# One graph-network kernel, one core: gathers gated per tile and on the preparation's products, window one-hots made in smaller pieces

## The reference, cut to what matters

```python
# first layer: relational graph convolution
msg = sum_b (x[src] @ weight[b]) * w_comp[etype][:, b]        # 8 bases
agg = relu(segment_sum(msg * norm, dst) + bias)
x1  = layernorm(x + agg)
# second layer: messages with edge features, then an MLP with batch norm
neigh = segment_sum(x1[src] + edge_feat, dst)
h   = relu(batchnorm(((1 + eps) * x1 + neigh) @ W1 + b1))
out = layernorm(x1 + h @ W2 + b2)
```

## Time and profile before

| | us |
|---|---|
| median of 3 runs (780.35 to 783.78) | 781.75 |
| the profiled execution, its own time | 781.48 |
| its span in the trace | 779.7 |

### The profile page before, as it was taken

The page is one execution under the profiler, slowest core; times in us unless marked ns, Lnnn a source line. Parts: engine busy times, 40 slices in busy tenths (PEclk is TensorE's granted clock), DMA queues, the critical chain, the costliest instruction groups (busy, mean ns, idle before and its releaser), DMA issues.

```text
span 779.7 us, 13302 instructions
## 1 busy us (share of the span) xinstructions
PE 585.2 (75%) x3971; PEld 480.7 (62%) x3971; DVE 493.7 (63%) x1866; ACT 297.0 (38%) x672; POOL 418.9 (54%) x434
## 2 busy tenths in 40 slices
PE   4137877777878686888678877797787876999994
PEld 2025766655667574776556766666676665878764
DVE  7039666667569676777764887767774344536456
ACT  9502444544455444445443544345340000000074
POOL 6730767667667665766765666666656666100000
PEclk9998657677875788757889788999889888999998
DMA  4400335455454654545744647566565562463002
GB/s 115 108 25 2 99 117 147 119 158 149 133 145 119 189 170 149 163 131 161 217 134 126 203 136 221 167 200 200 153 199 161 181 203 71 126 240 129 2 1 83
DMA packets 97035, 108.21 MB, mean 139 GB/s; under 512 B 10805, under 2 KB 81446, under 8 KB 96962
## 3 DMA queue, kind: packets, MB, share of 16 engines
q1 hardware_dynamic: 80898, 79.25, 32.6%
q0 software_dynamic: 13312, 27.29, 12.8%
q10 hardware_dynamic: 2752, 0.79, 0.4%
HBM read 81.73 MB, written 25.56 MB: 138 GB/s over the span
## 4 chain that ended last, share of the span: by engine, by line
DVE 34%; PE 34%; another core or an unknown queue 12%; issue 10%; DVEq 4%; ACT 3%; DMA 1%; ACTq 0%; SPq 0%
PE psum L1053 11%; DVE etype_hot L1388 7%; PE psum L999 6%; DVE etype_hot L1385 5%; PE psum L1029 5%; PE psum L1005 5%; DVE sums_flat L1509 5%; PE psum L1020 3%; DVE adj_flat L1479 3%; DVE weighted L1307 3%; DVE adj_flat L1283 2%; DVEq L1482 1%; ACT adj_flat L804 1%; DVE sums_flat L1463 1%
## 5 line engine op out<-in xcount | busy, mean ns | idle before, releaser
L716 POOL DMA_INDIRECT gathered_flat<-in_x_dram,src_i x416 | 416.6, 1001 | 247.3 <-issue 106.2
L999 PE MATMUL psum<-weighted,gathered_flat 128*128 128x160 f32 (+1 forms) x832 | 178.0, 342 | 23.4 <-issue 21.0
L999 PEld LDWEIGHTS psum<-weighted,gathered_flat 128*128 128x128 f32 x832 | 156.6, 238 | 42.1 <-issue 39.7
L1509 DVE TENSOR_TENSOR sums_flat<-psum,sums_flat 128x180 f32 x208 | 71.9, 346 | 168.8 <-remote 90.8
L1020 PE MATMUL psum<-etype_hot 128*128 128x300 f16 (+2 forms) x624 | 119.2, 313 | 48.4 <-issue 26.2
L778 ACT ACTIVATE adj_flat<-zero_col 128x450 f16<-128x450 f32 x208 | 108.4, 579 | 107.9 <-DMA adjacency<-adj_flat 66.6
L1005 PEld LDWEIGHTS psum<-hot,attrs 128*128 128x128 f32 x832 | 136.5, 231 | 9.5 <-issue 9.4
L1005 PE MATMUL psum<-hot,attrs 128*128 128x20 f32 (+1 forms) x832 | 131.0, 273 | 7.7 <-issue 7.7
L1388 DVE TENSOR_SCALAR etype_hot<-iota_key,key_t 128x300 f16<-128x300 f16 (+1 forms) x416 | 131.9, 318 | 0.0
L1020 PEld LDWEIGHTS psum<-etype_hot 128*128 128x128 f16 x624 | 69.7, 132 | 68.9 <-issue 43.0
L1385 DVE TENSOR_SCALAR etype_hot<-iota_key,gathered_flat 128x128 f16<-128x128 f16 x416 | 108.8, 262 | 0.1
(11 more groups left out here) (144 smaller groups left out, 345.6 us busy)
## 6 DMA issues: line engine op xcount, KB each, us to landing
attrs<-in_edge_attr_dram SPq DMA_DIRECT2D x51, 512.0 KB
adjacency<-adj_flat SPq DMA_DIRECT2D x26, 900.0 KB
sums_flat<-adjacency SPq DMA_DIRECT2D x13, 576.0 KB
gathered_flat<-in_x_dram,src_i POOLq DMA_INDIRECT x416
coef<-adjacency SPq DMA_DIRECT2D x23, 288.0 KB
sums_flat<-adjacency SPq DMA_DIRECT2D x5, 648.0 KB, 8.8
sums_flat<-adjacency SPq DMA_DIRECT2D x9, 288.0 KB
out_dram<-gathered_flat SPq DMA_DIRECT2D x6, 256.0 KB
```

The costliest lines, as they stand in the source:

```text
L716: pool.indirect_dma_start(gathered[:, t % (RING * GROUP), :], None, x[:, :], bass.IndirectOffsetOnAxis(src_i[:, t:t + 1], 0)).then_inc(gat ...
L999: nc.tensor.matmul(ps[:, 0:B, STARTS[i]:STARTS[i] + WIDTHS[i]], gathered[:, (u * UNIT + i) % (RING * GROUP), 0:F], weighted_tiles(s, i)[:, ...
L1509: nc.vector.tensor_tensor(window, unit_psum(u), window, ALU.add).then_inc(added, 1)
```

## The change

Four edits. (1) In the preparation POOL's gathers of units 8 to 15 each wait for a number of finished coefficient quads: 26 (u - 7) // 8, that is 3, 6, 9, ... 26. (2) In the main loop each gather waits for its own tile: each tile's gather product (L999) adds one to a new semaphore `tiles_read`, and the gather of tile t waits for t - 31 of them. (3) DVE makes place one-hots for a couple (2 tiles per instruction) and weighted ones for a unit (1 tile per instruction), spread over the couples: after couple w the ones of couple w + 4, between the halves of the keys. (4) `select_ready` counts units, PE waits for it at each unit, and SP's waits are scaled to it.

```diff
@@ sync: loads into coef
-                        sp.wait_ge(select_ready, (place - NEARS - FARS + 1) * FREE_COEF)
+                        sp.wait_ge(select_ready, (place - NEARS - FARS + 1) * FREE_COEF * GU)
...
-                        sp.wait_ge(select_ready, GROUPS)
+                        sp.wait_ge(select_ready, U)
@@ gpsimd
             def gather_unit(u):
 
-                if u >= RU:
-                    pool.wait_ge(sums_mm, (u - RU) // 2 + 1)
                 for t in range(u * UNIT, (u + 1) * UNIT):
+                    if u >= RU:
+                        pool.wait_ge(tiles_read, t - RU * UNIT + 1)
                     pool.indirect_dma_start(
...
             for u in range(RU):
+                if u >= RU // 2:
+                    pool.wait_ge(coef_mm, QUADS * (u + 1 - RU // 2) // (RU // 2))
                 gather_unit(u)
@@ tensor: sums_of_unit
-                        pe.wait_ge(select_ready, g + 1)
+                    pe.wait_ge(select_ready, u + 1)
...
-                                         start=(i == 0), stop=(i == UNIT - 1))
+                                         start=(i == 0), stop=(i == UNIT - 1)).then_inc(tiles_read, 1)
@@ vector
-            def places_hot(g, s):
-
+            def places_hot(w):
+
+                g, lo = 2 * w // GU, 2 * w % GU
                 for i, n in enumerate(WIDTHS):
+                    t = 2 * w * UNIT + i
                     last = nc.vector.tensor_tensor(
-                        hot_tiles(s % 2, i),
-                        rel_t[:, g * GROUP + i:(g + 1) * GROUP:UNIT].unsqueeze(2).to_broadcast([P, HALF, n]),
-                        iota_win[:, 0:n].unsqueeze(1).to_broadcast([P, HALF, n]), ALU.is_equal)
+                        hot_tiles(g % 2, i)[:, lo:lo + 2, :],
+                        rel_t[:, t:t + 2 * UNIT - i:UNIT].unsqueeze(2).to_broadcast([P, 2, n]),
+                        iota_win[:, 0:n].unsqueeze(1).to_broadcast([P, 2, n]), ALU.is_equal)
                 last.then_inc(hot_ready, 1)
 
-            def weight_hot(g, s):
-
-                dve.wait_ge(hot_ready, g + 1)
+            def weight_hot(u):
+
+                g, j = u // GU, u % GU
+                dve.wait_ge(hot_ready, u // 2 + 1)
                 for i, n in enumerate(WIDTHS):
+                    t = u * UNIT + i
                     last = nc.vector.tensor_tensor(
-                        weighted_tiles(s % 2, i), hot_tiles(s % 2, i).unsqueeze(2).to_broadcast([P, HALF, B, n]),
-                        coef[:, g * GROUP + i:(g + 1) * GROUP:UNIT, :].unsqueeze(3).to_broadcast([P, HALF, B, n]),
+                        weighted_tiles(g % 2, i)[:, j, :, :], hot_tiles(g % 2, i)[:, j, :].unsqueeze(1).to_broadcast([P, B, n]),
+                        coef[:, t:t + 1, :].rearrange("p t b -> p (t b)").unsqueeze(2).to_broadcast([P, B, n]),
                         ALU.mult)
                 last.then_inc(select_ready, 1)
...
-            for g in range(2):
-                places_hot(g, g)
-                weight_hot(g, g)
+            for w in range(GU):
+                places_hot(w)
+                for u in range(2 * w, 2 * w + 2):
+                    weight_hot(u)
...
-                    for c in range(min(U, counted(2 * w - 2) + KEYRING), min(U, counted(2 * w) + KEYRING)):
-                        keys_hot(c)
+                    if w + GU < COUPLES:
+                        places_hot(w + GU)
+                    fresh = range(min(U, counted(2 * w - 2) + KEYRING), min(U, counted(2 * w) + KEYRING))
+                    for j in range(2):
+                        for c in fresh[:(len(fresh) + 1) // 2] if j == 0 else fresh[(len(fresh) + 1) // 2:]:
+                            keys_hot(c)
+                        if w + GU < COUPLES:
+                            weight_hot(2 * (w + GU) + j)
...
-                    if w % 2 == 1 and g + 2 < GROUPS:
-                        places_hot(g + 2, g)
-                        weight_hot(g + 2, g)
```

More of the change, by code:

```diff
@@ L406, in gnn_resnorm_kernel @@
         sums_mm = sem("sums_mm")
+        tiles_read = sem("tiles_read")
         added = sem("added")
```

## The result

On the chip of the first measurement the changed kernel takes 778.66 us (median of 13 runs, 774.6 to 784.0), the kernel before 783.10 (13 runs). The ratio is 0.9946 [0.9924, 0.9968]: 4.4 us faster, where 28 were forecast. The profiled execution took 777.41 us, its span is 775.6.

The account below looks back on a forecast made before the run. The prediction took POOL's back-to-back gathers, which hold back PE's reports, to set the main loop's beat. Its terms, -16 + 1 - 27 + 14 = -28 us from 781.5, gave 753.5 us, with a range of 712 to 782.

Parts of the forecast that it names:

- (3) The wait per tile: Main loop: each gather waiting for its own tile lengthens gather runs to 11.6, so fewer stops; -27 us.
- (2) The first one-hots: Start of PE's block products: first unit about 1 us sooner, but the keys behind its one-hots later; +1 us.
- (4) The smaller pieces: DVE in the main loop: more, smaller one-hot instructions add 23 to 57 us of work, mostly covered by idling; +14 us.
- (1) The gate: Preparation: gathers 17 to 32 waiting for quads let PE's reports through earlier; -16 us, ends 10 and 22.
- Rival (d): Preparation: the gate does nothing, late gathers hold the quads just as long and only shift; 781 us, chance 0.07.
- rival (c): Main loop: POOL wakes at the first report, so runs get short and the kernel slower; 802 us, chance 0.11.
- Rival (a): Only the preparation gains; in the main loop DVE's extra work eats what POOL gains; 766 us, chance 0.20.
- (b): Main loop: single-tile waits free PE's reports often enough that half of the 107 us of stops goes; 711 us, chance 0.15.

Follow-up runs that it names:

- split_3: Kernel before with only the smaller one-hots at their earlier place in the couple, and the matching waits: 794.5 us against 774.7, ratio 1.0249.
- gate_3: Kernel before with only the preparation's gathers 17 to 32 waiting for coefficient quads: 758.8 us against 774.7, ratio 0.9807.
- tile_3: Kernel before with only the main loop's wait per tile: 767.2 us against 774.7, ratio 0.9897.
- no_gather: Kernel before without the main loop's gathers, PE multiplying the rows the preparation brought: 690.7 us against 780.2, ratio 0.8848.
- gate_2: Kernel before with only the preparation's gathers 17 to 32 waiting for coefficient quads, on a faster chip: 667.1 us against 667.7, ratio 0.9988.
- tile_only: Kernel before with only the main loop's wait per tile, on a faster chip: 666.8 us against 666.6, ratio 1.0008.
- tile_2: Kernel before with only the main loop's wait per tile, again on a faster chip: 666.2 us against 667.7, ratio 0.9966.
- group_early: Kernel before with its group-sized one-hots, unchanged, moved ahead of keys, block additions and shared columns: 784.4 us against 775.1, ratio 1.0114; repeated, 1.0150.
- split_last: Kernel before with the smaller one-hots, placed at the couple's end where the group-sized ones stood: 784.4 us against 775.1, ratio 1.0113.

## Why the prediction was wrong

Its direction was right and its size was not: 4.4 us for 28, the profiled run 777.4 for 753.5. Of the 24 us between them, about 20 are term (3) and 5 are terms (2) and (4) together. By its own terms, for chips of kind B:

**(1) The gate, -16: right.** Alone it measures -15.9. The quads resumed at 29 us (DVE's row after its last wait, 29.23 in the trace of after), the pairs recurred each 3.3 us instead of the feared 4.1, and the first product moved by 18.8 us, between the ends of 10 and 22. Rival (d) is out. On kind A, where there is no hold, the same edit gives nothing.

**(2) The first one-hots, +1: about right.** The first product came a little sooner (70.98 for 72.44 us in split_3), but the second unit 5.6 us after it (53.65, 59.25), where gate_3 has 3.3:

```profile
53.60 1.29 PE L1001 MATMUL psum<-weighted,gathered_flat 128*128 128x160 f32 x4 [3.27 <-DVE weighted L1309]
...
56.85 1.19 PE L1001 MATMUL psum<-weighted,gathered_flat 128*128 128x160 f32 x4
```

That is 1.5 us sooner and 2.3 later; in time it is part of the split's 19.8.

**(3) The wait per tile, -27: the step that failed.** It measures -7.5 on kind B and nothing on kind A. The step took a run of gathers plus a stop as the beat of the loop, filled the run up with the tiles that the old wait rounds away, to 11.6, and called the rest gain. The runs did not fill up: in tile_3 they are 5.2 gathers long (5.9 before), and the stops stayed at 110 us (for 106.5). POOL woke sooner to fewer credits, as rival (c) said.

One number of the step was read in the wrong place. "2.26 us a unit" is the spacing of 77.95 and 80.21, where the granted clock is 0.50 (stretch of 77 to 82 us); later in the same run of gathers, at 1.00 (84 to 88 us), PE's units follow each other by 1.2 us:

```profile
84.70 0.66 PE L999 MATMUL psum<-weighted,gathered_flat 128*128 128x160 f32 x4
...
85.88 0.66 PE L999 MATMUL psum<-weighted,gathered_flat 128*128 128x160 f32 x4
```

Why (c) came without its price has an answer in its own sum. It puts a run of n at 1.29 n + 1.3 us, 6.5 us for four, but the row that it cites has four in 6.1 us, 1.53 a tile, which is the mean of the loop before. Runs of 5.2 are above its own limit of 4.5, too.

The premise of the step, "the main loop runs in a beat set by POOL", is weaker for it, though no run decides on it alone. If POOL has 384 gathers of 1.25 us to place in 588 us, it idles for some 107 us whatever it waits for, so the sum of its stops doesn't tell that it is the bound. What the gathers cost the rest is 90 us in no_gather, and the wait per tile won 7.5 of them. Nor is there one wait that stands for the loss: the "remote" ahead of DVE's additions, 90.8 us before, is 64.4 in tile_3, but also 66.9 in split_3, which is 20 us slower than before. So the step that failed is known, the length of the runs; by which waits the late reports cost the loop its time stays open.

The Trainium skill's 26 ns per increment ("TensorE: Matmul & The Clock Gate", "The cost: per-tile semaphore tail"), 11 us here by an estimate from that page, doesn't show: on kind A, where the stops are few (12 in gate_2), tile_only and tile_2 are at 1.0008 and 0.9966, and 11 us would be 1.7%. Counting nothing was right there; on kind B it can't be told apart from the gain.

**(4) The smaller pieces, +14: mis-sized.** With term (2), so for a forecast of +15, they measure +19.8 (the upper end of (4) was 20), and +44 us on kind A. Two errors partly cancelled. The work was over-estimated: the durations came out as forecast, 162.6 us for the four forms against 100.1 of the four before, 62.5 more; but neighbours overlap, and DVE's busy time rose by 28.4 only, near the lower end of 23. The Trainium skill's fixed part of 58 cycles ("VectorE: DVE Perf Modes", "The TRN2 errata") gave 25 us by an estimate from that page, nearer the busy time than the 57 from the rows' means. And the effect of that work was under-estimated: not 0.35 of it but 0.7 on kind B (19.8 of 28.4) and 1.6 on kind A (44.6 of 28). The share of DVE in the chain says nothing of where in DVE's order work is put in. About half the price is the place: group_early, with not one instruction more, costs 9 and 11 us on kind B, split_last 9, the two together about the 19.8; on kind A the place is 29 of 45. (On kind B the group-sized pieces stand for the small ones; no small pieces were measured at both places on one chip there.) The prediction let the lead of four couples stand for "needed by nobody yet" and did not ask what stands behind the moved one-hots on DVE: the block additions and the shared columns.

Rival (a), only the preparation gains (766), with DVE's extra work eating what POOL gains, was nearest in mechanism; the loop did not stay equal, though, but lost 14.7 us, as the split costs more than the wait per tile wins. (c)'s short runs came without the loss it priced, (b) did not occur. The range held the time because it was wide (712 to 782): the terms inside it were 24 us off together.

The best version is the change without its smaller one-hots: 0.9690 and 0.9688 of before on kind B, about 3% ahead of the changed kernel. On kind A that combination was not run; its two parts alone are level with before. The changed kernel was not run on kind A either; without its wait per tile (no_tile) it loses 45 us there.

## What to carry to other kernels

An engine that stops regularly looks like the bound, but it has to stop somewhere if it has less work than time; before pricing its stops, work out from rows at several places of the loop whether the edit would really make them fewer. Work moved earlier on an engine's queue costs what stands behind it and is needed now, even if the engine has a third of its time idle; so try work with long lead last. Where a profile shows a large share of waits on an unknown queue, measure on a second chip before building on it.

## What the runs showed of the hardware

The same kernel took 667 us on two chips and 775 to 783 us on the others. The difference goes with POOL's indirect gathers: with them left out of the loop, the kernel takes 690.7 us instead of 780.2 on a chip of the slower kind, with a loop of 616 us, and the granted clock averages 0.88 instead of 0.83. In the trace the mark is the releaser "remote" on engines that wait for PE; on the other kind the eight kernels run there have none (the kernel before was timed there, not profiled). In the preparation it is as plain: the first product is at 72.4 us on kind B without the gate, 53.6 with it, and 42 on kind A with or without. What in the chips makes the difference, and how long a pause of POOL lets reports through, stays open. In the preparation the pauses seen to do it were of 0.97 to 1.18 us (after), while those of 0.30 us did not (before); in the loop of before, stops as short as 0.72 us ended with a report too.
